# Attention on one Trainium2 core: GpSimd takes over the joining of queries and keys and the causal zeroing, and TensorE's second mask is replaced by two filler matmuls

## Time and profile before

| what | value |
|---|---|
| median of 3 runs | 725.33 us (724.91 to 726.94) |
| the profiled execution's own time | 727.6 us |
| its span in the profile | 725.8 us |
| busy in the span: PE, DVE, ACT, POOL | 631.4, 579.9, 477.5, 200.9 us |
| granted TensorE clock, mean | 0.93 |
| attention's 32 steps | from about 50 to about 206 us |

### The profile page before, as it was taken

One profiled execution on the slowest core, in us unless ns is written; L12 is line 12 of the kernel. 1 busy time (PEld: TensorE's weight loads), 2 busy tenths in 40 slices (PEclk: granted clock), 3 DMA queues, 4 the chain that ended last, 5 costly groups with the idle time before them and its releaser, 6 DMA issues.

```text
span 725.8 us, 11354 instructions
## 1 busy us (share of the span) xinstructions
PE 631.4 (87%) x3252; PEld 435.9 (60%) x3252; DVE 579.9 (80%) x1400; ACT 477.5 (66%) x843; POOL 200.9 (28%) x160
## 2 busy tenths in 40 slices
PE   8689899999997899999999995755997988999983
PEld 5355555555545578888888883332665855666762
DVE  2669999999866668888888977649897788888887
ACT  5438888888644579999999994594452534444441
POOL 3400000000002315455435434201422133444423
PEclk9679999999996999999999999785997999999996
DMA  6000000000000212102222100000000321111111
GB/s 224 30 0 2 2 2 0 0 0 0 1 1 0 89 61 88 61 28 87 87 88 87 59 21 0 23 0 0 1 0 4 139 80 65 72 58 60 66 59 58
DMA packets 6796, 30.88 MB, mean 43 GB/s; under 512 B 906, under 2 KB 1043, under 8 KB 4435
## 3 DMA queue, kind: packets, MB, share of 16 engines
q1 hardware_dynamic: 6756, 30.42, 11.6%
HBM read 29.23 MB, written 1.19 MB: 42 GB/s over the span
## 4 chain that ended last, share of the span: by engine, by line
PE 52%; DVE 25%; issue 11%; ACT 10%; DVEq 1%; DMA 1%; POOL 0%; ACTq 0%; SPq 0%
PE PS L1051 10%; PE PS L1053 10%; PE PS L1052 10%; DVE AR L1021 6%; DVE STAT L741 5%; ACT RA L576 4%; PE PS L1166 2%; PE PS L1064 2%; PE PS L1128 2%; DVE HN L600 2%; PE PS L1193 2%; PE PS L1148 2%; PE PS L1073 2%; PE PS L1162 2%; PE PS L1127 1%
## 5 line engine op out<-in xcount | busy, mean ns | idle before, releaser
L297 POOL TENSOR_TENSOR AR<-AR 128x512 f32<-128x512 f32 x68 | 100.9, 1483 | 228.2 <-DVE AR L687 227.6
L875 DVE TENSOR_TENSOR RA<-AR,RA 128x512 fp32r<-128x512 f32 x140 | 135.3, 992 | 29.7 <-ACT RA L481 28.8
L480 ACT ACTIVATE AR<-PS,BI 128x512 f32<-128x512 f32 x144 | 99.5, 691 | 23.9 <-PE PS L1053 14.0
L1051 PE MATMUL PS<-HH,WH 128*128 128x512 f32 x272 | 108.8, 400 | 1.5 <-DVE AR L1021 1.5
L1052 PE MATMUL PS<-HH,WL 128*128 128x512 f32 x272 | 107.8, 396 | 0.0
L1053 PE MATMUL PS<-HL,WH 128*128 128x512 f32 x272 | 107.7, 396 | 0.0
L1051 PE MATMUL PS<-RA,WH 128*128 128x512 f32 x208 | 86.9, 418 | 17.9 <-DVE RA L1028 17.2
L576 ACT ACTIVATE RA<-AR 128x512 fp32r<-128x512 f32 x64 | 40.5, 633 | 89.9 <-DVE AR L1021 89.9
L481 ACT ACTIVATE RA<-PS,BI 128x512 fp32r<-128x512 f32 x144 | 98.4, 684 | 0.0
L1028 DVE TENSOR_TENSOR RA<-AR,RA 128x512 fp32r<-128x512 f32 x64 | 72.2, 1128 | 27.6 <-ACT RA L576 24.7
L1053 PE MATMUL PS<-RA,WH 128*128 128x512 f32 x208 | 82.2, 395 | 0.0
(11 more groups left out here) (183 smaller groups left out, 1197.7 us busy)
## 6 DMA issues: line engine op xcount, KB each, us to landing
AR<-comb SPq DMA_DIRECT2D x17, 1024.0 KB, 4.6
WS<-in_w SPq DMA_DIRECT2D x9, 512.0 KB, 5.5
WS<-in_w SPq DMA_DIRECT2D x8, 384.0 KB, 4.9
M<-in_mats SPq DMA_DIRECT2D x1, 1384.0 KB, 12.1
X<-in_xT SPq DMA_DIRECT2D x4, 256.0 KB, 4.4
out_xT<-X SPq DMA_DIRECT2D x4, 256.0 KB, 2.1
AR<-in_wmod SPq DMA_DIRECT2D x1, 768.0 KB, 9.0
KM<-in_kmats SPq DMA_DIRECT2D x1, 160.0 KB, 9.5
```

The source lines that it names most:

```text
L297: gp.tensor_tensor(out=blk(ACC, t), in0=blk(ACC, t), in1=YW[:, t % 2, :], op=ALU.add)\
L480: act.activation(G[:, c, :], PS[:, c, :], ACT.Gelu_apprx_tanh, bias=bias).then_inc(s["act"], 1)
L875: dve.tensor_tensor(out=GL[:, m0 % 2, c, :], in0=G[:, c, :], in1=f(GH[:, m0 % 2, c, :]), op=ALU.subtract).then_inc(s["lo"], 1)
L1051: pe.matmul(out, wh, xh, start=first, stop=False)
```

```diff
-            for m in (IDF, IDB, MQ, MKK, MP):
+            for m in (IDF, IDB, MQ, MP):
...
+            def causal(n, n0):
+                for h in range(2):
+                    gp.wait_ge(exp_done, 2 * n + h + 1)
+                    own = PR[:, n0 % 2, 2 * h:2 * h + 2, :]
+                    for first in (0, 256):
+                        p = own[:, :, first:first + 128]
+                        ins = gp.affine_select(out=p, in_=p, compare_op=ALU.is_ge, fill=none, base=0,
+                                               pattern=[[0, 2], [1, 128]], channel_multiplier=-1)
+                    ins.then_inc(causal_done, 1)
+            def join(n):
+                gp.wait_ge(qk_evac, 4 * n + 4)
+                if n >= 4:
+                    gp.wait_ge(st_done, 2 * n - 6)
+                gp.tensor_tensor(out=QKX[:, n % 4, :, :], in0=QKT[:, :, :], in1=f(QKR), op=ALU.add)\
+                  .then_inc(qx_ready, 2)
+            for n in range(3):
+                join(n)
+            for n in range(UNITS):
+                causal(n, n)
+                if n + 3 < UNITS:
+                    join(n + 3)
             gp.wait_ge(moe[0]["w_in"], 16)
             split_weights(0, 0, 0, 1024)
...
-                act.activation(QT[:, :], PS[:, 6, 0:256], ACT.Identity, bias=vec("bq", g)).then_inc(qk_evac, 1)
-                act.activation(KT[:, :], PS[:, 6, 256:512], ACT.Identity, bias=vec("bk", g)).then_inc(qk_evac, 1)
-                act.wait_ge(qk_evac, 4 * n + 2)
-                act.activation(QR, QT[:, :], ACT.Copy, scale=vec("q_sign")).then_inc(qk_evac, 1)
-                act.activation(KR, KT[:, :], ACT.Copy, scale=vec("k_sign")).then_inc(qk_evac, 1)
+                for i, name in enumerate(("q", "k")):
+                    act.activation(QKT[:, i, :], PS[:, 6, 256 * i:256 * i + 256], ACT.Identity,
+                                   bias=KEPT[:, i, g:g + 1], scale=vec(name + "_keep")).then_inc(qk_evac, 1)
+                    act.activation(QKR[:, i, :], PS[:, 6, 256 * i:256 * i + 256], ACT.Identity,
+                                   bias=SIGNED[:, i, g:g + 1], scale=vec(name + "_sign")).then_inc(qk_evac, 1)
...
-                dve.tensor_copy(NMH, NM[:, :]).then_inc(nmh_done, 1)
-                dve.wait_ge(nmh_done, n + 1)
                 if n0 >= 1:
                     dve.wait_ge(mt_done, n)
-                dve.tensor_copy(MP[:, :, 24::32], f(NMH).rearrange("p (q j) -> p q j", q=2)).then_inc(mp_ready, 1)
-                dve.tensor_tensor(out=MP[:, :, 25::32], in0=nmv, in1=f(NMH).rearrange("p (q j) -> p q j", q=2),
+                dve.tensor_copy(MP[:, :, 24::32], nmv).then_inc(mp_ready, 1)
+                dve.wait_ge(mp_ready, 2 * n + 1)
+                dve.tensor_tensor(out=f(MP[:, :, 25::32]), in0=nmv, in1=f(MP[:, :, 24::32]),
                                   op=ALU.subtract).then_inc(mp_ready, 1)
...
-                if n0 + 3 < UNITS:
-                    join(n + 3, (n0 + 3) % 4)
-                else:
+                if n0 + 3 >= UNITS:
                     attended(n0 - 29)
...
             def project(n, n0, it):
                 if n0 >= 1:
                     pe.wait_ge(qk_evac, 4 * n)
+                if n0 >= 3:
+                    keep_clock(2, 6)
...
-                for j in range(2):
-                    mm = pe.matmul(diagonal(2 + 2 * h + j), IDB[:, :], mask(MKK), start=False, stop=True)
                 mm.then_inc(st_done, 1)

             def values(n, n0, it):
-                pe.wait_ge(exp_done, 2 * n + 2)
+                pe.wait_ge(causal_done, 2 * n + 2)
```

More of the change, by code:

```diff
@@ L245, in _ @@
             gp.memset(OND[:, :], 1.0 / D).then_inc(const_done, 1)
-            for m in (IDF, IDB, MQ, MKK, MP):
-                gp.memset(m[:], 0.0).then_inc(ident_done, 1)
-            gp.wait_ge(ident_done, 5)
+            for m in (IDF, IDB, MQ, MP):
+                gp.memset(f(m[:]) if m is MP else m[:], 0.0).then_inc(ident_done, 1)
+            gp.wait_ge(ident_done, 4)
             for m in (IDF, IDB):
@@ L400, in evac_proj @@
             def evac_proj(n, g):
+                if isinstance(n, int) and n == 0:
+                    act.wait_ge(qk_bias, 4)
                 act.wait_ge(proj_done, n + 1)
@@ L720, in all_values @@
                    .then_inc(vall_done, 1)
-            def join(n, g):
-                dve.wait_ge(qk_evac, 4 * n + 4)
-                if not isinstance(n, int) or n >= 4:
-                    dve.wait_ge(st_done, 2 * n - 6)
-                dve.scalar_tensor_tensor(out=QX[:, g, :], in0=QT[:, :], scalar=vec("q_keep"), in1=f(QR),
-                                         op0=ALU.mult, op1=ALU.add).then_inc(qx_ready, 1)
-                dve.scalar_tensor_tensor(out=KX[:, g, :], in0=KT[:, :], scalar=vec("k_keep"), in1=f(KR),
-                                         op0=ALU.mult, op1=ALU.add).then_inc(qx_ready, 1)
             nmv = NM[:, :].rearrange("p (q j) -> p q j", q=2)
@@ L809, in step @@
                     maxima(n + 2, n0 + 2, 0)
-                if n0 + 3 < UNITS:
-                    join(n + 3, (n0 + 3) % 4)
-                else:
+                if n0 + 3 >= UNITS:
                     attended(n0 - 29)
+            for i, name in enumerate(("q", "k")):
+                bias = V[:, VAT["b" + name]:VAT["b" + name] + 4]
+                dve.tensor_scalar(KEPT[:, i, :], bias, vec(name + "_keep"), None, ALU.mult).then_inc(qk_bias, 1)
+                dve.tensor_scalar(SIGNED[:, i, :], bias, vec(name + "_sign"), None, ALU.mult).then_inc(qk_bias, 1)
             dve.wait_ge(sp_done, 3)
@@ L819, in _ @@
             dve.tensor_scalar(SP[:, 3:4], SP[:, 3:4], -8.0, None, ALU.mult).then_inc(sp_done, 1)
-            dve.wait_ge(ident_done, 9)
+            dve.wait_ge(ident_done, 7)
             dve.wait_ge(in_rows, 32)
-            join(0, 0)
             all_values(0)
@@ L828, in _ @@
             spread_max(0, 0)
-            join(1, 1)
             with_max(0, 0)
@@ L835, in _ @@
             maxima(1, 1, 0)
-            join(2, 2)
             for n in range(4):
@@ L1120, in _, with keep_clock @@
                   .then_inc(kd_done, 1)
+            def keep_clock(count, bank=7):
+                for _ in range(count):
+                    pe.matmul(PS[:, bank, :], LH[:, 0:128], LH[:, 0:512], start=True, stop=True)
             def project(n, n0, it):
@@ L1220, in step @@
                     values(n - 1, n0 - 1, it)
-            def keep_clock(count, bank=7):
-                for _ in range(count):
-                    pe.matmul(PS[:, bank, :], LH[:, 0:128], LH[:, 0:512], start=True, stop=True)
             pe.wait_ge(in_k, 16)
```

34 lines of the change are left out of this document (17 added, 17 removed).

## The result

The changed kernel takes **747.07 us** (median of 4 executions, 745.94 to 754.67) beside 725.12 us for the kernel before in the same series (723.02 to 726.94). The ratio is 1.0326, 95% interval 1.0252 to 1.0400: slower, where the prediction had 719.8 us and a range up to 737. The mean granted clock is 0.871 to 0.888 in all four executions, and the profiled one shows that TensorE's clock falls in attention, so that is the kernel's own time.

The account below looks back on a forecast made before the run. PE's and DVE's coupled 4.73 us loops bound attention. Terms -2.3 (29 steps), -2.0, -2.0, +0.3 and +0.5 sum to -5.5 us: 719.8 us against the 725.33 median, range 713 to 737.

Parts of the forecast that it names:

- the fourth rival: TensorE's clock falls in attention; even one 10 us stretch costs some 4 us; chance 0.05, nearly all slower.
- The loops: Attention step: PE's and DVE's loops both sum to 4.73 us, so gaining on one alone is worth nothing.
- rival 1: Attention: POOL's selects and DVE's operations miss each other; step is PE's 4.52 us, time 716.0 us; chance 0.20.
- Mask and filler: PE's loop in attention: removing mask matmuls gives -0.66 us a step, two fillers add +0.45, leaving 4.52.
- Select 0.41 and join 1.3 to 1.5: POOL's own time in attention, us per operation; 3.1 a step, within 4.5, so POOL by itself costs nothing.
- What POOL does to DVE: Attention: DVE operations wait for POOL's selects, 0.2 us a step, making DVE's loop and the step 4.65.
- one meeting: Attention: DVE waits once a step for half a select, 0.2 us; the divide behind the subtraction should not wait again.
- rival 2: Attention: cast and subtraction each wait for POOL, together about 0.45 us; step 4.90, time 727.0 us; chance 0.18.
- rival 3: Attention: cast, subtraction and divide each wait for selects, 0.8 us; step 5.25, time 737.2 us; chance 0.22.
- Before attention: Expert 0's weight split no longer delays DVE: -2.0 us (-1.2 to -3.0); first join on POOL, less one ACT wait: +0.3.
- Steps 29 to 31: Last attention steps lose the mask and get no filler, PE being the longer side: 3 x -0.66 = -2.0 us.
- Behind attention: The weight split now runs after the last selects and delays DVE's L792: +0.5 us (0 to +1).

Follow-up runs that it names:

- Join alone: Changed kernel without selects and fillers, mask matmuls back on PE, leaving join and row maximum moved and POOL's queue changed: 723.20 us, ratio 0.9988.

## Why the prediction was wrong

**The step that failed is the fourth rival, "the clock falls", at a chance of 0.05, so that the sum had nothing for it.** In the profiled execution the clock fell twice, and that cost 26.4 + 6.2 = 32.6 us. The price of a low step was near by luck: PE's 2.56 us would "grow to about 5", which with the 0.91 and 1.26 of its loop makes some 7.2, and 6.99 was measured; but at the low clock PE has no wait left (78.40 us busy of 78.40), so that a step is PE's whole stream and not a part of it and two waits. The prediction named both conditions, the filler shorter than the mask and PE waiting where POOL delays DVE. What was wrong was the argument against this rival, that the fillers use all rows of the array: at 1024 columns two fp32r matmuls let the clock fall in 4 of 4 executions, where bf16 ones of as many columns held it. And for a fall in every execution both conditions are needed. Without selects the clock holds with the fp32r fillers (713.79 us), with selects after `with_max` it holds with them too (717.98), and with bf16 fillers and the selects in their old place it holds in 15 of 17 executions. Neither repair makes a fall impossible: with fp32r fillers and no work on POOL one of 4 executions fell. The clock of 1.00 in the earlier trace rows was taken as a margin, and one trace can't show that: the kernel before itself has a mean clock of 0.82 to 0.83 in 23 of 68 executions. Why the type counts stays open.

Point by point:

- **The loops.** Half right. Join alone gives nothing (4.74) and both without selects 4.49 in most steps (rival 1 had 4.52 for PE's loop). But "a gain on one is worth nothing without one on the other" fails for PE: with the join still on DVE, fillers for masks took the step to 4.62. Two sums of starts once round a step both come to 4.73 whatever bounds the step, so they could not show that the loops are equally long.
- **Mask and filler, -0.66 and +0.45.** The difference was right: from 4.73 with the mask (join alone) to 4.49 with fillers (no selects) is -0.24, forecast -0.21. The single terms were not. The two fillers take 0.57 from start to start (66.27 to 66.84), and the mask took 0.80: from the scores to the projection it was 70.55 - 69.14 = 1.41 us before, and from the scores to the fillers it is 61.60 - 60.99 = 0.61 after.

```profile
69.14 0.33 PE L1148 MATMUL PS<-RA 32*128 32x128 f32 x2 [0.26 <-DVE NM L741]
70.55 0.60 PE L1127 MATMUL PS<-HN,M 128*128 x2
```

```profile
60.99 0.33 PE L1170 MATMUL PS<-RA 32*128 32x128 f32 x2 [0.27 <-DVE NM L758]
61.60 0.73 PE L1141 MATMUL PS<-LH 128*128 128x512 f32 x2
```

- **Select 0.41 and join 1.3 to 1.5.** Measured 0.408 and 1.279 at the median; with the selects after `with_max` the step is the one without selects (4.53), so POOL by itself cost nothing.
- **What POOL does to DVE, 0.2 in the mean.** Right in the mean, in part by luck: step 4.67, forecast 4.65, before 4.73 and (185.70 - 52.75) / 28 = 4.75 from transposes to transposes. But "one meeting" is not what happens. In some steps only the subtraction waits (+0.12) and the step is 4.50, as in rival 1; in 7 of 13 the cast waits as well (about 0.23 and 0.15 together with the subtraction's in the rows above), and the step is 4.68 to 4.78, on the way to rival 2. So two operations in a row can each be stopped by a block of selects; the divide as the third was not. The copies of `place_values` (+0.23 in a pair) were not in the sum; without them held, PE's rest in a fourth step is 0.42 and not 0.64. The rule of the Trainium skill ("SBUF — State Buffer", "SBUF: two separate sides"), that VectorE and GpSimd lock the shared ports for a whole instruction, agrees with the trace: a cast of 8 elements took up to 411 ns beside a select where 174 is its own time. The Trainium skill ("VectorE: DVE Perf Modes", "Mode 2×_2P") also says that a copy within SBUF can use both read ports, and the trace agrees in that the copies wait too (444 ns for 218). Three waits a step (rival 3, 0.8) were not seen.
- **Before attention, -1.7 with the first join.** Transposes of unit 1 stand at 49.82 where they stood at 52.75: -2.9. In the 15 traced versions of the changed kernel they lie between 47.5 and 51.1, and in the kernel before with fillers for masks at 51.8, so a gain is clear (some 3 us in the mean, an estimate from these starts) and the single number isn't better known than that.
- **Steps 29 to 31, -2.0.** Mis-sized. The last two steps take 6.75 and 6.62 us where they took 7.05 and 6.96: about -0.6. At some 7 us they are much longer than the others, which the prediction, with no row of them, did not look at; no run was made on them either.
- **Behind attention, +0.5.** L808 took 1.70 for 0.69: +1.0, the upper end. It does not show in the whole: from the last transposes to the end the profiled executions take between 523 and 527 us, before 526.5, the change 526.7.

At a held clock the sum is near the measured time: the three versions with bf16 fillers and the selects in their old place, whose steps are 4.66 and 4.67 in the mean ((180.71 - 50.17) / 28 = 4.66 with LH), give 718.42 to 719.82 us for a forecast of 719.8. Here too more before attention and less in steps 29 to 31 cancel. The prediction had the steps right in the mean and was wrong about the clock at which they run.

## What to carry to other kernels

- Matmuls that look like spare work can be what keeps TensorE's clock up. Whoever replaces matmuls by others should count a change of type as a risk, at equal columns too, and read the clock row first: the falls cost 32.6 us in the profiled execution of the change, and the whole change at a held clock is worth some 7.
- Work that moves to GpSimd should be placed in time, and not only in the queue: behind an operation of VectorE that reads PSUM it cost nothing, in front of a cast, copies and two-input operations it cost waits and, here, with fp32r fillers, the clock.
- In coupled loops one half of a change can measure as nothing and still be needed for the whole (join alone 0.1%, fillers for masks 0.5%, both without selects 1.4%); measure both halves together before dropping either.

## What was unexpected of the hardware

- **The type of the filler.** With the selects in their old place 1024 columns of fp32r (0.57 us) did not hold the clock in any of 8 executions, and 1024 of bf16 (0.45 us) did in 15 of 17, although PE is then busy less. Why, no run here shows.
- **A low clock that stays under full load.** From 71.4 to 149.8 us PE's records leave no gap (78.40 of 78.40) and the granted clock is 0.50 all the time; then it rises, with the same kind of steps before and behind it. Without fillers it lasts 153.6 us. The Trainium skill ("TensorE: Matmul & The Clock Gate", "What's actually happening") says that activity releases the throttle; here records without a gap went on for 78 us at the low clock, and what ends the low stretch stays open.
- **The mask's version is not safe either.** By time and mean clock the kernel before fell in 23 of 68 executions (9 of the 25 beside the version with joins on POOL), the one with the split moved in 2 of 10, the one with joins on POOL in 0 of 10. No trace of such an execution was kept, so where its clock is low is not shown, nor was it tried further whether the join on POOL lowers that share.
